# Attention weights on ScalarE: each half's logarithm followed at once by that half's two exponentials

## The chip, the cores and the metric

The kernel runs on one core of a Trainium2 chip. The metric is the device time of one execution in microseconds (us), given as the median of several runs of the same kernel. A profile of one execution stands beside it: the trace shows when each engine worked, what it worked on and what ended its waits.

## What is computed

The program takes x of 16 sequences, 256 tokens and 128 channels through four layers, each behind a layer norm and with a residual: a Mamba block, a mixture of experts, an attention, and the experts again. The change lies in the attention. It has 16 heads of 8 channels and weighs keys by inverse squared distance, not by a softmax:

```python
sq = q2 + jnp.swapaxes(k2, -1, -2) - 2.0 * jnp.einsum('bhqd,bhkd->bhqk', Q, K)
dist = jnp.sqrt(jnp.maximum(sq, 0.0))
W = (SHEP_EPS + dist) ** (-SHEP_P)          # SHEP_EPS = 1e-4, SHEP_P = 2
W = W / (SHEP_EPS + jnp.sum(W, axis=-1, keepdims=True))
return jnp.einsum('bhqk,bhkd->bhqd', W, V)
```

So for each of the 16 sequences there are 16 heads times 256 times 256 numbers to go through a square root and a power of -2. The kernel takes the power as exp(-2 ln(dist + eps)).

## The kernel before, in words

The layers run one after the other, with a barrier of all engines between them. Each engine has its own instruction list, written out by hand; what sets the order between engines are semaphores, and within an engine the order of the code.

The attention layer handles one sequence (a batch in the code) per turn, 16 turns, in a software pipeline. While turn b runs, TensorE (PE) computes the scores of the 16 heads of sequence b+1, one head at a time (`score`, L1295), into two PSUM buffers `s_ps`. VectorE (DVE) reads each into SBUF as a squared distance (`distance`, L1461), in the buffer `d`, which has two halves p and 1-p for alternate sequences. After heads 7, 11 and 15 DVE raises `d_ready`. ScalarE (ACT) meanwhile turns the distances of sequence b, which lie in the other half of `d`, into weights, in place. PE multiplies finished weights by the values (`weigh`, L1303), four heads at a time: the weighing of the first three groups stands in PE's list behind the scores of heads 13, 14 and 15, and that of the fourth behind head 1 of the next turn. Each waits for one more count of `w_done`, which ACT raises once per finished group. What follows (transposes L1312 and L1318, the division by the sum and the gate on DVE, the output projection L1324, the update of x at L1497) is spread over the heads of the next turn.

ACT's work of one turn is short: three square roots (heads 0 to 7, 8 to 11, 12 to 15; L1384), a load of the function table that holds both logarithm and exponential (L1385), two logarithms of 8 heads each (L1388), and four exponentials of 4 heads each (L1392), each of which raises `w_done`. The table of the square root is loaded again at the head of the next turn. ACT signals itself with `act_chain`: the three square roots raise it to 3, the two logarithms to 5, and an instruction that reads what an earlier one wrote waits for that count. On ACT no DMA is issued in this layer.

For the last sequence there are no further scores to compute: PE does the four groups, then two rounds of transposes and the projection, and the layer ends with DVE's update of x.

Another place that the prediction uses is the softplus of the Mamba layer (L486 to L488): three ACT instructions in a row, of which each reads what the one before it wrote and waits for its semaphore.

Of the kernel before, what the change touches and what calls it, by code (L numbers as in the profile page):

```python
# [23 lines left out]
ACT = mybir.ActivationFunctionType  # L24
# [14 lines left out]
HG = 4  # L39
# [24 lines left out]
def take(eng, sem, n=1):  # L64

    eng.wait_ge(sem, n)
    eng.sem_inc(sem, -n)  # L67
# [1034 lines left out]
def attention_layer(nc, sems, x_sb, aw, loaded, ident, ident16, half):  # L1102

    ctx = ExitStack()
    with ctx:
# [6 lines left out]
        def sem(name):  # L1112
            return sems.enter_context(nc.semaphore("a_" + name))
# [38 lines left out]
        pool_chain, dve_chain, act_chain, d_chain = sem("pool_chain"), sem("dve_chain"), sem("act_chain"), sem("d_chain")  # L1152
# [4 lines left out]
        s_ready, s_free, d_ready, w_done = sem("s_ready"), sem("s_free"), sem("d_ready"), sem("w_done")  # L1157
# [3 lines left out]
        def batches(eng, body, prologue, epilogue):  # L1161


            prologue()
            body(-1, 1, core=False, tail=False)
            body(0, 0, tail=False)
            with eng.Fori(0, NB // 2 - 2) as i:
                body(i * 2 + 1, 1)
                body(i * 2 + 2, 0)
            body(NB - 3, 1, further=False)  # L1170
            body(NB - 2, 0, further=False, ahead=False)
            body(NB - 1, 1, further=False, ahead=False, heads=False)
            epilogue()
# [10 lines left out]
        @block.sync  # L1184
        def _(sp):
            sp.wait_ge(loaded["attention"], 16 * len(aw.NAMES))
            for s in w_ready.values():
                sp.sem_inc(s, 1)
# [184 lines left out]
        @block.scalar  # L1373
        def _(act):
            def body(b, p, core=True, tail=True, heads=True, ahead=True, further=True):

                def heads_of(first, n):
                    return d[:, p, first:first + n].rearrange("p h k -> p (h k)")

                if not core:  # L1380
                    return
                for first, n in ((0, 8), (8, 4), (12, 4)):
                    take(act, d_ready)
                    nc.scalar.activation(heads_of(first, n), heads_of(first, n), ACT.Sqrt).then_inc(act_chain, 1)  # L1384
                nc.scalar.preload_act_table_set("natural_log_exp_and_others")  # L1385
                for half in range(2):
                    act.wait_ge(act_chain, 1 + 2 * half)
                    nc.scalar.activation(heads_of(8 * half, 8), heads_of(8 * half, 8), ACT.Ln, bias=near[:, 0:1]).then_inc(act_chain, 1)  # L1388
                for g in range(HG):
                    if g % 2 == 0:  # L1390
                        act.wait_ge(act_chain, g // 2 + 4)
                    nc.scalar.activation(heads_of(4 * g, 4), heads_of(4 * g, 4), ACT.Exp, scale=-2.0).then_inc(w_done, 1)  # L1392
                act.sem_inc(act_chain, -5)

            act.wait_ge(near_made, 1)
            batches(act, body, lambda: None, lambda: None)
# [262 lines left out]
```

## Time and profile before

| what | us |
|---|---|
| runs, median | 1593.68 |
| runs, all three | 1593.68, 1592.61, 1593.71 |
| the profiled execution, device time | 1592.62 |
| its span in the profile | 1590.9 |
| busy in that span: PE | 1308.6 |
| DVE | 1273.3 |
| ACT | 1097.2 |
| POOL (GpSimd) | 897.1 |

The span runs from the first instruction of the program to the last; 1.7 us of the device time lie around it. The shares of busy time are means over four layers that are limited by different things. The attention layer lies at about 850 to 1278 us of the span, between the two expert layers.

### The profile page before, as it was taken

Reading aid. Unit: us, or ns where it says so; the run is one execution under the profiler, and the core shown is the slowest. Engines: PE = TensorE matmul, PEld = TensorE weight load, DVE = VectorE, ACT = ScalarE, POOL = GpSimd, SP = SyncE. Lnnn points to the kernel's source line nnn. Section 1 sums busy time; section 2 is a strip of 40 time slices with the busy share of each in tenths; the row PEclk is TensorE's granted clock in tenths of the full one; section 3 lists DMA queues with packets and bytes.
Section 4 is the critical chain, followed back from the end, with each engine's and each line's share of the span. In section 5 each row is a group of like instructions: output and inputs, shape, how many; then the busy total and the mean of one; then the engine's idle time right before and its main releaser. Section 6 shows DMA issues by size and latency. Waiting matters only on the chain. (4 is left out here: it accounts for less than half of the span.)

```text
span 1590.9 us, 21353 instructions
## 1 busy us (share of the span) xinstructions
PE 1308.6 (82%) x6384; PEld 626.4 (39%) x6384; DVE 1273.3 (80%) x2163; ACT 1097.2 (69%) x1578; POOL 897.1 (56%) x1052
## 2 busy tenths in 40 slices
PE   4688888888886499999994777778878569999998
PEld 3344444444442244444441233333333224444443
DVE  2899999999999678878864788888887357877775
ACT  4667767867866255555550899999999935555554
POOL 5898888889877365555554322322321025555555
PEclk8899999999999799999996577867766569999999
DMA  7122122122110132222220000000000022223330
GB/s 239 54 80 81 53 71 88 53 69 91 53 70 37 77 137 108 107 106 106 106 107 0 1 1 0 0 0 0 0 0 1 1 107 114 114 113 126 149 149 35
DMA packets 27923, 111.54 MB, mean 70 GB/s; under 512 B 4049, under 2 KB 9570, under 8 KB 19426
## 3 DMA queue, kind: packets, MB, share of 16 engines
q1 hardware_dynamic: 27010, 110.21, 18.5%
q10 hardware_dynamic: 864, 0.74, 0.1%
q8 instruction: 22, 0.36, 0.1%
q14 instruction: 27, 0.22, 0.0%
HBM read 108.06 MB, written 2.88 MB: 70 GB/s over the span
## 5 line engine op out<-in xcount | busy, mean ns | idle before, releaser
L845 POOL TENSOR_TENSOR e_h_lo<-e_h,e_h_hi 128x512 f16<-128x512 f32 x272 | 314.7, 1157 | 273.3 <-ACT e_h_hi L961 262.2
L270 POOL TENSOR_TENSOR m_h<-m_b_sb,m_dx 128x512 f32<-128x512 f32 x256 | 345.0, 1374 | 49.1 <-POOLq L67 40.4
L498 ACT ACTIVATE m_decay<-m_delta,mw_a_log 128x255 f32<-128x255 f32 x448 | 185.3, 461 | 119.4 <-DVEq L648 119.2
L643 DVE TENSOR_TENSOR_SCAN m_h<-m_decay,m_h 128x1024 f32<-128x1024 f32 x112 | 255.8, 2284 | 13.2 <-DVEq L60 7.5
L1056 DVE TENSOR_TENSOR e_cu<-e_u,e_c_bc 128x512 f32<-128x512 f32 x256 | 175.9, 687 | 108.7 <-PE e_u L885 87.5
L956 ACT ACTIVATE e_g<-e_g 128x512 f32<-128x512 f32 x256 | 149.1, 582 | 162.8 <-PE e_g L885 162.8
L374 PE MATMUL m_y_ps<-m_hc,ident 128*128 128x512 f32 x512 | 250.4, 613 | 0.0
L885 PE MATMUL e_g<-e_x_hi,ew_gate_up 128*128 128x512 f16 x544 | 210.2, 386 | 9.4 <-ACTq L960 9.4
L1461 DVE TENSOR_SCALAR a_d<-a_s 128x512 f32<-128x512 f32 x256 | 170.3, 686 | 56.7 <-PE a_s L1295 36.8
L885 PE MATMUL e_u<-e_x_hi,ew_gate_up 128*128 128x512 f16 x544 | 209.2, 385 | 0.0
L892 PE MATMUL e_y<-e_h_hi,ew_down 128*128 128x512 f16 x544 | 206.9, 381 | 1.6 <-POOL e_h_lo L845 1.6
L961 ACT ACTIVATE e_h_hi<-e_h 128x512 f16<-128x512 f32 x272 | 169.5, 623 | 55.7 <-DVE e_h L1061 54.9
L1061 DVE TENSOR_TENSOR e_h<-e_g,e_cu 128x512 f32<-128x512 f32 x256 | 176.9, 691 | 15.9 <-DVE e_cu L1056 1.1
L598 DVE TENSOR_TENSOR m_hc<-m_h,m_c_ps 128x1024 f32<-128x1024 f32 x128 | 152.8, 1194 | 0.6 <-PE m_c_ps L369 0.6
L1295 PE MATMUL a_s<-a_qkT 32*128 32x256 f16 x512 | 105.6, 341 | 57.7 <-DVE a_d L1461 42.8
L374 PEld LDWEIGHTS m_y_ps<-m_hc,ident 128*128 128x128 f32 x512 | 92.8, 197 | 73.0 <-issue 70.4
L1384 ACT ACTIVATE a_d<-a_d 128x2048 f32<-128x2048 f32 (+1 forms) x48 | 115.7, 2469 | 5.7 <-ACTq L67 5.5
L369 PE MATMUL m_c_ps<-m_bc,m_pick 96*128 96x256 f16 x256 | 49.4, 274 | 83.0 <-DVE m_hc L598 72.4
L1388 ACT ACTIVATE a_d<-a_d,a_near 128x4096 f32<-128x4096 f32 x32 | 116.9, 3701 | 0.2
L1392 ACT ACTIVATE a_d<-a_d 128x2048 f32<-128x2048 f32 x64 | 116.7, 1894 | 0.0
L885 PE MATMUL e_g<-e_x_lo,ew_gate_up 128*128 128x512 f16 x272 | 105.1, 386 | 0.0
L885 PE MATMUL e_u<-e_x_lo,ew_gate_up 128*128 128x512 f16 x272 | 104.6, 385 | 0.0
(190 smaller groups left out, 1999.5 us busy)
## 6 DMA issues: line engine op xcount, KB each, us to landing
e_c_bc<-mix SPq DMA_DIRECT2D x64, 1024.0 KB, 6.8
m_b_sb<-b_rows SPq DMA_DIRECT2D x64, 512.0 KB, 5.4
ew_gate_up<-w_gate_up SPq DMA_DIRECT2D x1, 2176.0 KB, 13.5
out<-x_sb SPq DMA_DIRECT2D x8, 256.0 KB, 2.3
ew_down<-w_down SPq DMA_DIRECT2D x1, 1088.0 KB, 11.5
mw_conv_rows<-w_conv_rows ACTq DMA_DIRECT2D x1, 640.0 KB
mix<-e_cT SPq DMA_DIRECT2D x16, 32.0 KB, 1.6
x_sb<-x SPq DMA_DIRECT2D x1, 256.0 KB, 3.1
```

Of the source, the lines that this page charges most:

```text
L270: ins = nc.gpsimd.tensor_tensor(h[:, m % 4, :, c], b_sb[:, p, 2 * m:2 * m + 2], dx[:, p, c:c + 1].to_broadcast([P, 2, T]), ALU.mult)
L374: ins = nc.tensor.matmul(y_ps[:], ident[:], hc[:, m % 2, n].rearrange("p c t -> p (c t)"), start=(m == 0 and n == 0), stop=(m == PAIRS - 1 ...
L498: ins = nc.scalar.activation(decay_of(m, p)[:, at + 1:at + T], delta[:, p, c, 1:T], ACT.Exp, scale=neg_a[:, c, 2 * m + n:2 * m + n + 1])
L598: nc.vector.tensor_tensor(hc[:, m % 2], h[:, m % 4], c4, ALU.mult).then_inc(hc_ready, 1)
L643: nc.vector.tensor_tensor_scan(flat, decay_of(m, p)[:], flat, 0.0, ALU.mult, ALU.add).then_inc(scan_chain, 1)
L845: nc.gpsimd.tensor_tensor(h_lo[:, k], h[:, k], h_hi[:, k], ALU.subtract).then_inc(h_lo_ready, 1)
L885: ins = nc.tensor.matmul(ps[bank][:], ew.gate_up[r][:, e, side], a[:, p], start=(n == 0), stop=(n == 2))
L892: ins = nc.tensor.matmul(y_ps[:], ew.down[r][:, e], a[:, place(e)], start=(e == 0 and n == 0), stop=(e == NE and n == 2))
L961: nc.scalar.activation(h_hi[:, place(e)], h[:, place(e)], ACT.Copy).then_inc(h_hi_ready, 1)
L1056: nc.vector.tensor_tensor(cu[:, e % 2], u_ps[bank][:], c_bc[:, e], ALU.mult).then_inc(core_chain, 1)
L1061: nc.vector.tensor_tensor(h[:, place(e)], g_ps[bank][:], cu[:, e % 2], ALU.mult).then_inc(h_ready, 1)
L1461: ins = nc.vector.tensor_scalar(d[:, p, h], s_ps[h % 2][:], -2.0, 0.0, ALU.mult, ALU.max)
```

## The change

In each turn ACT issued logarithm 0, logarithm 1, exponentials 0, 1, 2, 3. Now it issues logarithm 0, exponentials 0 and 1, logarithm 1, exponentials 2 and 3. The instructions, their shapes, their number and the table loads are the same; only the place of the second logarithm among them is another. The counts of `act_chain` that are waited for stay: 4 (first logarithm done) ahead of exponential 0 and 5 (second logarithm done) ahead of exponential 2.

```diff
                 for half in range(2):
-                    act.wait_ge(act_chain, 1 + 2 * half)
+                    act.wait_ge(act_chain, (1, 3)[half])
                     nc.scalar.activation(heads_of(8 * half, 8), heads_of(8 * half, 8), ACT.Ln, bias=near[:, 0:1]).then_inc(act_chain, 1)
-                for g in range(HG):
-                    if g % 2 == 0:
-                        act.wait_ge(act_chain, g // 2 + 4)
-                    nc.scalar.activation(heads_of(4 * g, 4), heads_of(4 * g, 4), ACT.Exp, scale=-2.0).then_inc(w_done, 1)
+                    act.wait_ge(act_chain, 4 + half)
+                    for g in (2 * half, 2 * half + 1):
+                        nc.scalar.activation(heads_of(4 * g, 4), heads_of(4 * g, 4), ACT.Exp, scale=-2.0).then_inc(w_done, 1)
                 act.sem_inc(act_chain, -5)
```

ACT's list of one turn inside the loop, before; L1384 are the square roots, L1388 the logarithms, L1392 the exponentials, and `a_d` is the buffer `d`:

```order
L1384 ACT_TABLE_LOAD [waits a_d_ready]
L1384 ACTIVATE a_d<-a_d 128x4096
L1384 ACTIVATE a_d<-a_d 128x2048 [waits a_d_ready] x2
L1385 ACT_TABLE_LOAD
L1388 ACTIVATE a_d<-a_d,a_near 128x4096 [waits a_act_chain] x2
L1392 ACTIVATE a_d<-a_d 128x2048 [waits a_act_chain]
L1392 ACTIVATE a_d<-a_d 128x2048
```

The other two exponentials follow there in the same form. The same turn after the change, where the exponentials are line 1391:

```order
L1384 ACT_TABLE_LOAD [waits a_d_ready]
L1384 ACTIVATE a_d<-a_d 128x4096
L1384 ACTIVATE a_d<-a_d 128x2048 [waits a_d_ready] x2
L1385 ACT_TABLE_LOAD
L1388 ACTIVATE a_d<-a_d,a_near 128x4096 [waits a_act_chain]
L1391 ACTIVATE a_d<-a_d 128x2048 [waits a_act_chain]
L1391 ACTIVATE a_d<-a_d 128x2048
L1388 ACTIVATE a_d<-a_d,a_near 128x4096 [waits a_act_chain]
L1391 ACTIVATE a_d<-a_d 128x2048 [waits a_act_chain]
L1391 ACTIVATE a_d<-a_d 128x2048
```

The second logarithm has moved behind the first two exponentials, and each logarithm now stands directly ahead of an exponential that reads its result. No table load has come in.

PE's list at the end of the layer, for the last sequence, which the change leaves as it was:

```order
L1303 MATMUL a_av<-a_d,a_v 32x256 [waits a_v_ready,a_w_done]
L1303 MATMUL a_av<-a_d,a_v 32x256 x7
L1303 MATMUL a_av<-a_d,a_v 32x256 [waits a_w_done]
L1303 MATMUL a_av<-a_d,a_v 32x256 x7
L1303 MATMUL a_av<-a_d,a_v 32x256 [waits a_w_done]
L1303 MATMUL a_av<-a_d,a_v 32x256 x7
L1303 MATMUL a_av<-a_d,a_v 32x256 [waits a_w_done]
L1303 MATMUL a_av<-a_d,a_v 32x256 x7
L1312 MATMUL a_u<-ident,a_avT 128x128 [waits a_avT_ready]
```

The four groups wait for one count of `w_done` each, so the first two can now start when ACT has done half of the sequence, and the last two as before, behind the last two exponentials.

## Rows read from the trace of the kernel before

**Rows 1.** The page: span, and busy time with share and instructions of each engine.

```profile
span 1590.9 us, 21353 instructions
PE 1308.6 (82%) x6384; PEld 626.4 (39%) x6384; DVE 1273.3 (80%) x2163; ACT 1097.2 (69%) x1578; POOL 897.1 (56%) x1052
```

**Rows 2.** Busy time by stretch, the attention's steady part; columns in the first line.

```profile
core 0: us, PE busy (x) PEld busy (x) DVE busy (x) ACT busy (x) POOL busy (x), PEclk, DMA share, GB/s
890.00:1265.00 375.00, 287.32 (x1958) 123.27 (x1959) 293.83 (x649) 374.10 (x170) 97.93 (x219) 0.70 0.00 0
```

**Rows 3.** Timeline of ACT, one turn: start, duration, operation, count, idle before it.

```profile
930.69 7.22 ACT L1384 ACTIVATE a_d<-a_d 128x4096 f32<-128x4096 f32 x3
...
939.22 7.31 ACT L1388 ACTIVATE a_d<-a_d,a_near 128x4096 f32<-128x4096 f32 x2
946.43 7.29 ACT L1392 ACTIVATE a_d<-a_d 128x2048 f32<-128x2048 f32 x4
953.75 1.28 ACT L1384 ACT_TABLE_LOAD   x1
```

**Rows 4.** Groups by shape on ACT: count, busy us, mean ns of one, idle before.

```profile
L1388 ACT ACTIVATE a_d<-a_d,a_near 128x4096 f32<-128x4096 f32 x32 | 116.9, 3701 | 0.2
L1392 ACT ACTIVATE a_d<-a_d 128x2048 f32<-128x2048 f32 x64 | 116.7, 1894 | 0.0
...
L488 ACT ACTIVATE m_sp<-m_sp 128x512 f32<-128x512 f32 x16 | 10.1, 631 | 0.5
```

**Rows 5.** Timeline of ACT in the Mamba layer: one softplus, its two dependent instructions.

```profile
32.81 0.63 ACT L487 ACTIVATE m_sp<-m_sp 128x512 f32<-128x512 f32 x1
33.47 0.63 ACT L488 ACTIVATE m_sp<-m_sp 128x512 f32<-128x512 f32 x1
```

**Rows 6.** Waits, 900 to 1270 us: who for whom, us in total, times, longest.

```profile
PE a_av L1303 <- ACT a_d L1392: 14.1, 6, 9.4
```

**Rows 7.** Timelines of ACT and DVE, second turn: third square root and its input.

```profile
906.33 7.22 ACT L1384 ACTIVATE a_d<-a_d 128x4096 f32<-128x4096 f32 x3
...
908.27 0.69 DVE L1461 TENSOR_SCALAR a_d<-a_s 128x512 f32<-128x512 f32 x1 [0.23 <-PE a_s L1295]
```

**Rows 8.** Timeline, end of the attention layer: the last sequence on ACT, PE and DVE.

```profile
1255.81 7.31 ACT L1388 ACTIVATE a_d<-a_d,a_near 128x4096 f32<-128x4096 f32 x2
1263.03 7.29 ACT L1392 ACTIVATE a_d<-a_d 128x2048 f32<-128x2048 f32 x4
1264.97 5.11 PE L1303 MATMUL a_av<-a_d,a_v 128*32 128x256 f32 x48 [9.40 <-ACT a_d L1392]
...
1270.37 1.07 PE L1303 MATMUL a_av<-a_d,a_v 128*32 128x256 f32 x16 [0.29 <-ACT a_d L1392]
...
1272.46 1.06 PE L1312 MATMUL a_u<-ident,a_avT 128*128 128x128 f32 x8 [1.02 <-PEq L67]
...
1275.38 0.41 PE L1318 MATMUL a_u<-ident,a_o 128*128 128x128 f32 x2 [1.85 <-PEq L67]
...
1276.51 1.19 PE L1324 MATMUL a_u<-aw_attn_out_w,a_oT 128*128 128x128 f32 x4 [0.72 <-PEq L67]
```

**Rows 9.** Busy time by stretch at that end; granted TensorE clock stands behind POOL.

```profile
1268.00:1270.00 2.00, 2.00 (x24) 0.57 (x16) 0.69 (x1) 2.00 (x2) 0.00 (x0) 0.62 0.00 0
1270.00:1272.00 2.00, 1.15 (x20) 0.42 (x16) 0.38 (x1) 0.32 (x1) 0.00 (x0) 1.00 0.00 0
...
1276.00:1278.00 2.00, 1.19 (x4) 0.93 (x4) 0.40 (x2) 0.00 (x0) 0.00 (x0) 0.59 0.04 8
```

**Rows 10.** Timeline of PE: the same work at the other clock, in earlier turns.

```profile
915.40 1.94 PE L1312 MATMUL a_u<-ident,a_avT 128*128 128x128 f32 x8 [0.90 <-PEq L67]
...
974.06 0.68 PE L1324 MATMUL a_u<-aw_attn_out_w,a_oT 128*128 128x128 f32 x4
...
1143.21 1.93 PE L1303 MATMUL a_av<-a_d,a_v 128*32 128x256 f32 x16 [0.86 <-ACT a_d L1392]
...
1253.00 0.66 PE L1318 MATMUL a_u<-ident,a_o 128*128 128x128 f32 x2 [1.85 <-PEq L67]
```

## The prediction, made before the changed kernel was run

> **What bounds the kernel now.** The busy shares of the whole span come first, and they mislead: PE has 82%, DVE 80%, ACT 69% [rows 1]. The change touches one layer, so the second view is the busy time of that layer's steady stretch, 890 to 1265 us. There ACT works 374.10 of 375.00 us, DVE 293.83 and PE 287.32 [rows 2]: ACT bounds the attention, and its 0.9 us of idle time are small gaps around table loads. No DMA runs there (share 0.00). The third view is ACT's timeline over one turn [rows 3]: three square roots from 930.69, two logarithms from 939.22, four exponentials from 946.43, the next turn's table load right behind them at 953.75. The reader is to see that nothing between these rows is a wait for another engine; the turn of 24.35 us repeats to the end of the layer. The fourth view is who waits for ACT: PE waits at the weighing, 14.1 us in 6 waits, of which one of 9.4 is that of the last sequence [rows 6, 8]. So PE and DVE have time to spare in each turn and ACT has none. What the change does to ACT's own sequence is paid in full, and what it gives PE earlier is worth something only where PE makes ACT wait, or at the end of the layer.
>
> **The change part by part.** *What stays.* The 32 logarithms, 64 exponentials and 48 square roots, their shapes and the two table loads of a turn are the same, and the order of the changed program shows no load between a logarithm and an exponential. In the trace of before one load (L1385) already serves both [rows 3]. These edits cost nothing. The constant pair that replaces a formula gives the same counts.
>
> *What is added: two dependent starts in a turn.* Before, each logarithm was followed by an instruction that did not need it: logarithm 0 by logarithm 1, logarithm 1 by exponential 0, which reads what logarithm 0 wrote 3.6 us earlier. Now exponential 0 reads what the instruction directly ahead of it writes, and so does exponential 2. Behind these waiting instructions are queued on ACT the rest of the turn and all later turns.
>
> The price of an independent start: two logarithms take 7.31 us from the first start to the last end, and the exponential starts 946.43 - 939.22 = 7.21 us after the first start, so it starts 0.1 us ahead of the end of its predecessor [rows 3]. More sharply by sums: 32 logarithms of 3.701 us would fill 118.4 us, and they cover 116.9; 1.5 us over the 16 pairs is 0.096 us of overlap. The exponentials say the same: 64 times 1.894 is 121.2, they cover 116.7; 4.5 us over the 48 pairs is 0.094 [rows 4]. The price of a dependent start: in the softplus L488 reads what L487 wrote, and starts 33.47 - (32.81 + 0.63) = 0.03 us after its end [rows 5]; over 16 of them the idle time before L488 is 0.5 us, 0.031 each [rows 4]. That is the same engine, the same kind of instruction and the same way of waiting; only the size differs, 512 elements against 4096. So a dependent start costs 0.094 + 0.031 = 0.125 us more than an independent one. Two in each of 16 turns are 32, or **4.0 us on the path**. Bounds from the same rows: 32 x 0.094 = 3.0 if nothing but the overlap were lost, and 0 if a long instruction told its successor earlier than a short one does. I take 4.0, since both parts of it repeat through all their rows.
>
> *What is removed: PE's wait for the first weights.* Exponential 0 ends some 3.6 us earlier in the turn (a logarithm's 3.701 less an overlap), and with it the first two groups can be weighed earlier. On the path this is worth nothing as long as ACT is never short of distances. The tightest place is the second turn: DVE finishes head 15 at 908.27 + 0.69 = 908.96, and the third square root, which needs it, starts 7.22 - 1.89 = 5.33 us after 906.33, at 911.66 [rows 7, 4]. There are 2.7 us of slack, and the change can only widen them: PE reaches the scores of heads 14 and 15 behind weighings that now wait less. What is late next is the third group, whose exponential comes no earlier than before. PE's waits move to there: nothing gained, nothing lost.
>
> *The end of the layer.* Here the last sequence has a tail that nothing hides. The last exponential ends at 1263.03 + 7.29 = 1270.32 and PE begins the fourth group at 1270.37 [rows 8]: no backlog of the first three groups is left, so starting two of them earlier shortens nothing. But it moves PE's work, and PE's granted clock moves with it. Before, the three groups ran in one piece from 1264.97 (48 matmuls, 5.11 us); the clock was at 0.5 of full, 1.2 GHz, and rose within the slice 1268 to 1270, to 2.4 GHz from 1270 on; it fell within 1276 to 1278 [rows 8, 9]. So the fourth group (1.07 us), the transposes (1.06) and the two that follow (0.41) ran at the higher clock and the projection (1.19) at the lower. After the change the first two groups run about 3.6 us earlier, PE then rests until the third group is ready, and the rise may come later. If it comes too late for all three, they cost 1.93, 1.94 and 0.66 us [rows 10], that is 0.86 + 0.88 + 0.25 = 2.0 us more, and the fourth group starts 0.1 us later, since the slow third (1.93) outlasts the 1.8 us between two exponentials [rows 4]: +2.1. If the rise comes as before, 0. If a later rise also means a later fall, the projection takes 0.68 instead of 1.19 [rows 10]: -0.5. I take the middle case, in which the third and the fourth group run slowly (+1.0) and the later fall gives the projection back (-0.5): **+0.5 us**, with the ends -0.5 and +2.1.
>
> The sum against the profiled execution: 1592.62 + 4.0 + 0.5 = 1597.1 us. The runs of before lie at two levels, 1592.6 and 1593.7; the profiled execution is of the lower, the median 1593.68 of the upper, which gives 1598.2. I take the middle, **1597.7 us**, 4.5 us above the middle of the two levels.
>
> **The rivals.** *No cost for a dependent start* (not slower). If the overlap of a long logarithm does not depend on who reads it, or if ACT is told of the write before its end shows, the 4.0 us vanish and the time is 1592.6 to 1593.7, or up to 2.1 more with a slow tail. For it speaks only that no logarithm of 4096 elements is followed by its reader in the trace of before; against it the even 0.031 and 0.094 us [rows 4, 5]. It decides as soon as the cost of one start falls below 0.1 us: 32 of them are then within 3.2 us, which is 0.2% and about what a measurement of this kernel can tell from no change.
> The Trainium skill, in Advanced Engine Details and Errata under The Read-Write Bubble, says that on ScalarE the memory latency stands as a bubble between any two instructions, reader or not; by that rule the dependent start adds nothing, the sum is this rival's, and the trace disagrees, with 0.094 us of overlap in the one case and 0.031 of gap in the other.
>
> *PE sets the pace* (faster). If ACT's turns were in truth drawn along by PE's waits at the weighing, the waits other than the last sequence's, 14.1 - 9.4 = 4.7 us [rows 6], would go, and ACT's extra starts would lie in gaps: 1593.2 - 4.7 = 1588.5 us. It would need gaps on ACT ahead of its square roots. There are none in the steady stretch [rows 2, 3], so this has a small chance.
>
> *A cold tail* (slower still). The end of the layer runs wholly at the lower clock, +2.1 instead of +0.5: 1592.6 + 4.0 + 2.1 = 1598.7 to 1599.8. For it speaks that PE rests twice in the last sequence instead of once; against it that the third and fourth group, both slow, would follow each other without a pause, as the three groups did before the rise [rows 8, 9].
> The Trainium skill, in TensorE: Matmul & The Clock Gate under Part 1, says that the clock follows how busy the array has been of late; it speaks for this rival, and rows 9 agree in that the rise came in the midst of unbroken matmuls.
>
> *A reload of the table* at each change between logarithm and exponential can be left out: none stands in the new order.
>
> **How the numbers follow.** The forecast has 0.70, the cold tail 0.13, a start that costs nothing or too little 0.13, PE's pace 0.04. The first two are slower by over 0.2%: 0.83. The third is within 0.2%, 0.13, and the last faster, 0.04. The range goes from the lower level with the best tail and 0.3 us of scatter, 1592.6 + 4.0 - 0.5 - 0.3 = 1595.8, to the upper with the cold tail and 0.4 of scatter, 1593.7 + 4.0 + 2.1 + 0.4 = 1600.2, and leaves the last two cases out.
>
> **What would show it.** In the profile of after: ACT's turn is 24.60 us instead of 24.35; each logarithm is followed by idle time of 0.03 us, and the extent of two exponentials in a row stays 3.69; the steady stretch lasts 4 us longer with ACT still near 100% busy; PE's waits at the weighing stand before the third group and not the first. In the tail, the fourth group takes 1.07 or 1.93 us. The prediction is wrong if ACT's turn stays within 0.1 us of 24.35, if ACT shows waits ahead of its square roots, or if the expert layer behind it begins otherwise than shifted.

## The result and the profile after

The changed kernel takes 1598.36 us (median of 7 runs, 1597.46 to 1599.30), the kernel before 1592.95 us in the runs beside it (7 runs, 1592.61 to 1593.71). The ratio is 1.0033 with a 95% interval of 1.0021 to 1.0045: 5.4 us slower. The profiled execution took 1598.36 us with a span of 1596.6 us, 5.7 us more than before [rows 1].

The first view is ACT's timeline over the same turn as in rows 3: start, duration, operation, count. Line 1388 is the logarithm, 1391 now the exponential.

```profile
929.99 1.28 ACT L1384 ACT_TABLE_LOAD   x1
931.28 7.22 ACT L1384 ACTIVATE a_d<-a_d 128x4096 f32<-128x4096 f32 x3
938.52 1.28 ACT L1385 ACT_TABLE_LOAD   x1
939.81 3.71 ACT L1388 ACTIVATE a_d<-a_d,a_near 128x4096 f32<-128x4096 f32 x1
943.55 3.71 ACT L1391 ACTIVATE a_d<-a_d 128x2048 f32<-128x2048 f32 x2
947.17 3.70 ACT L1388 ACTIVATE a_d<-a_d,a_near 128x4096 f32<-128x4096 f32 x1
950.90 3.71 ACT L1391 ACTIVATE a_d<-a_d 128x2048 f32<-128x2048 f32 x2
954.63 1.28 ACT L1384 ACT_TABLE_LOAD   x1
```

From load to load the turn is 954.63 - 929.99 = 24.64 us, where it was 24.35 [rows 3]. The square roots and the loads are as long as before. The exponentials start 0.03 us after the end of their logarithm (939.81 + 3.71 = 943.52, then 943.55), and two exponentials in a row take 3.71 us instead of 3.69.

The second view is the groups by shape on ACT in the attention layer: count, busy us and mean ns of one, idle time before.

```profile
L1391 ACT ACTIVATE a_d<-a_d 128x2048 f32<-128x2048 f32 x64 | 118.7, 1902 | 1.0
L1388 ACT ACTIVATE a_d<-a_d,a_near 128x4096 f32<-128x4096 f32 x32 | 118.5, 3702 | 0.2
```

The 32 logarithms now cover 118.5 us, the sum of their single lengths, where they covered 116.9 [rows 4]. That alone does not show a lost overlap: the cover of a group counts only what its own members share, and the logarithms no longer stand side by side. (They cover 118.5 us as well in the experiment below that has this order without the waits.) What shows it are the starts: before, the first exponential started 0.1 us ahead of the end of the second logarithm [rows 3]; now each exponential behind a logarithm starts after its end. Before the 64 exponentials stands 1.0 us of idle time, 0.031 at each of the 32 that read their predecessor's result, and the mean of one has grown from 1894 to 1902 ns.

The third view is the busy time of the steady stretch, with the columns of rows 2, and PE's waits at the weighing over 900 to 1275 us.

```profile
890.00:1265.00 375.00, 285.88 (x1954) 122.94 (x1954) 293.43 (x650) 373.12 (x168) 97.93 (x219) 0.71 0.00 0
```

```profile
PE a_av L1303 <- ACT a_d L1391: 24.0, 17, 7.3
```

ACT is still busy for 373.12 of 375 us. PE's waits did not go away. There are more of them, 24.0 us in 17 waits, where there were 14.1 in 6 up to 1270 us [rows 6], and a look at one later turn shows where they now stand (timeline of PE, weighing alone):

```profile
1142.92 1.94 PE L1303 MATMUL a_av<-a_d,a_v 128*32 128x256 f32 x16
1145.32 1.51 PE L1303 MATMUL a_av<-a_d,a_v 128*32 128x256 f32 x16
1149.96 1.07 PE L1303 MATMUL a_av<-a_d,a_v 128*32 128x256 f32 x16 [1.82 <-ACT a_d L1391]
1151.76 1.07 PE L1303 MATMUL a_av<-a_d,a_v 128*32 128x256 f32 x16 [0.40 <-ACT a_d L1391]
```

The first two groups go through unheld, the third waits 1.82 us and the fourth 0.40. Before, the wait stood ahead of the first group [rows 10]. It does not leave that place everywhere: in five turns the first group waited before, and in two it still does, for 0.44 and 0.92 us.

The fourth view is the end of the layer, against rows 8 and 9: the last sequence on ACT, PE and DVE, and the granted clock by slices (it stands behind POOL's column). PEq and DVEq are the engines' own sequencers.

```profile
1271.17 3.71 ACT L1391 ACTIVATE a_d<-a_d 128x2048 f32<-128x2048 f32 x2
1273.13 3.35 PE L1303 MATMUL a_av<-a_d,a_v 128*32 128x256 f32 x32 [3.74 <-ACT a_d L1391]
...
1277.51 1.07 PE L1312 MATMUL a_u<-ident,a_avT 128*128 128x128 f32 x8 [1.03 <-PEq L67]
...
1280.43 0.66 PE L1318 MATMUL a_u<-ident,a_o 128*128 128x128 f32 x2 [1.85 <-PEq L67]
...
1281.81 1.19 PE L1324 MATMUL a_u<-aw_attn_out_w,a_oT 128*128 128x128 f32 x4 [0.72 <-PEq L67]
...
1283.26 0.42 DVE L1496 TENSOR_TENSOR x_sb<-a_u,x_sb 128x256 f32<-128x256 f32 x1 [1.60 <-DVEq L67]
```

```profile
1268.00:1270.00 2.00, 1.40 (x16) 0.39 (x8) 0.41 (x1) 2.00 (x1) 0.00 (x0) 0.72 0.00 0
1270.00:1272.00 2.00, 0.00 (x0) 0.00 (x0) 0.28 (x1) 1.97 (x2) 0.00 (x0) 1.00 0.00 0
1272.00:1274.00 2.00, 0.86 (x10) 0.41 (x14) 0.00 (x0) 2.00 (x2) 0.00 (x0) 0.64 0.00 0
1274.00:1276.00 2.00, 2.00 (x24) 0.78 (x20) 0.00 (x0) 0.88 (x1) 0.00 (x0) 0.51 0.00 0
1276.00:1278.00 2.00, 0.97 (x15) 0.52 (x6) 0.69 (x1) 0.00 (x0) 0.00 (x0) 1.00 0.00 0
1278.00:1280.00 2.00, 0.58 (x6) 0.34 (x4) 1.17 (x4) 0.00 (x0) 0.00 (x0) 0.84 0.00 0
```

The last exponential ends at 1271.17 + 3.71 = 1274.88 us instead of 1270.32 [rows 8]; the first logarithm of the layer started at 890.53 us and 890.51 before. So ACT's part of the layer is 4.54 us longer. From there the last update of x ends 1283.68 - 1274.88 = 8.80 us later; before it was 8.06. That makes 4.54 + 0.74 = 5.3 us. The other 0.4 us of the span's 5.7 lies in the last expert layer, which has nothing changed: from the last update of x to the end of the span there were 312.5 us before, 312.9 after, and between 312.8 and 313.3 in the traces of the experiments.

### The profile page after: what moved, and what is told of

The parts are those of the page before. It is cut to its first block and busy times, and to the rows that moved or that the text cites. A ratio compares the mean times of both kernels' runs of the same rounds, so it can differ in the third digit from the quotient of the medians.

```text
span 1596.6 us, 21353 instructions
## 1 busy us (share of the span) xinstructions
PE 1306.3 (82%) x6384; PEld 624.4 (39%) x6384; DVE 1273.1 (80%) x2163; ACT 1100.6 (69%) x1578; POOL 897.0 (56%) x1052
## 5 line engine op out<-in xcount | busy, mean ns | idle before, releaser
L1384 ACT ACTIVATE a_d<-a_d 128x2048 f32<-128x2048 f32 (+1 forms) x48 | 115.7, 2469 | 5.7 <-ACTq L67 5.5
L1391 ACT ACTIVATE a_d<-a_d 128x2048 f32<-128x2048 f32 x64 | 118.7, 1902 | 1.0
L1388 ACT ACTIVATE a_d<-a_d,a_near 128x4096 f32<-128x4096 f32 x32 | 118.5, 3702 | 0.2
L1303 PE MATMUL a_av<-a_d,a_v 128*32 128x256 f32 x1024 | 87.7, 474 | 24.0 <-ACT a_d L1391 24.0
```

## The experiments

The theory after this reading: the loss is the **dependent start**, an ACT instruction that waits for the one directly ahead of it. Two in a turn cost 0.284 us, 16 turns 4.54 us. The rival: it is the **new order**, through the moment at which PE gets weights, its clock, or anything else that moves with it. A third term is the end of the layer. The kernel before was run on the same chips beside each set: 1593.23 us (26 runs) for the first four experiments, 1592.27 us (21 runs) for the last two.

### The waits without the order

```diff
                 for half in range(2):
-                    act.wait_ge(act_chain, 1 + 2 * half)
+                    act.wait_ge(act_chain, 1 + 3 * half)
                     ...
                 for g in range(HG):
                     if g % 2 == 0:
-                        act.wait_ge(act_chain, g // 2 + 4)
+                        act.wait_ge(act_chain, 5)
```

> The order of before (both logarithms, then four exponentials), but logarithm 1 waits for logarithm 0 and exponential 0 waits for logarithm 1: two starts per turn that wait for their direct predecessor, with PE's work in the order and at the places of before. Theory 1 (the loss is the dependent start, 0.143 us each as the changed kernel's turn of 24.64 us against 24.35 shows): ACT's turn becomes 24.64 us, the layer 16 x 0.29 = 4.6 us longer, the end of the layer (last exponential to the last update of x) stays at 8.1 us as before; 1592.9 + 4.6 = 1597.5 us. Theory 2 (the loss comes from the new order: weights that are ready earlier move PE's work and its clock, and ACT's waits cost nothing): the turn stays at 24.35 us and the time at 1592.9.

Measured: 1597.40 us, ratio 1.0029 (1.0017 to 1.0040), 4.2 us over before. The timeline of ACT, one turn:

```profile
929.72 1.28 ACT L1384 ACT_TABLE_LOAD   x1
...
939.54 7.45 ACT L1388 ACTIVATE a_d<-a_d,a_near 128x4096 f32<-128x4096 f32 x2
947.03 7.31 ACT L1392 ACTIVATE a_d<-a_d 128x2048 f32<-128x2048 f32 x4
954.36 1.28 ACT L1384 ACT_TABLE_LOAD   x1
```

The turn is 24.64 us, as in the changed kernel, with PE's work where it was before. Two logarithms take 7.45 us instead of 7.31 [rows 3], and the first exponential starts after the end of the second and not ahead of it. The order is not needed for the loss; the waits alone make it. Nor is the reading needed: logarithm 1 works on other heads than logarithm 0, exponential 0 reads what logarithm 0 wrote, and neither touches what its direct predecessor writes. The cost comes with the wait for the direct predecessor.

### One dependent start instead of two

```diff
...
+                log(0)
+                act.wait_ge(act_chain, 4)
+                power(0)
+                log(1)
+                power(1)
+                act.wait_ge(act_chain, 5)
+                power(2)
+                power(3)
```

`log(half)` is one logarithm with its wait for the square roots, `power(g)` one exponential; these lines stand in the place of both loops, which are left out here.

> Order logarithm 0, exponential 0, logarithm 1, exponentials 1, 2, 3: exponential 0 still reads its direct predecessor, exponential 2 no longer does (exponential 1 stands between). One dependent start per turn instead of two. Theory 1: turn 24.35 + 0.143 = 24.50 us, 16 x 0.143 = 2.3 us over before, plus 0 to 0.8 at the end of the layer: 1595.2 to 1596.0 us. Theory 2 (order): the first weights come as early as in the changed kernel, the second 1.8 us later than before less one logarithm; the loss would stay near that of the changed kernel, 1597 to 1598.5.

Measured: 1595.85 us, ratio 1.0016 (1.0007 to 1.0025), 2.6 us over before. ACT's timeline:

```profile
929.86 1.28 ACT L1384 ACT_TABLE_LOAD   x1
...
939.68 3.71 ACT L1388 ACTIVATE a_d<-a_d,a_near 128x4096 f32<-128x4096 f32 x1
943.43 1.91 ACT L1391 ACTIVATE a_d<-a_d 128x2048 f32<-128x2048 f32 x1
945.24 3.69 ACT L1388 ACTIVATE a_d<-a_d,a_near 128x4096 f32<-128x4096 f32 x1
948.84 5.50 ACT L1391 ACTIVATE a_d<-a_d 128x2048 f32<-128x2048 f32 x3
954.36 1.28 ACT L1384 ACT_TABLE_LOAD   x1
```

The turn is 24.50 us. Exponential 0 starts 0.04 us after its logarithm's end and takes 1.91 us; behind the second logarithm the next one starts ahead of the end, at 948.84 against 945.24 + 3.69 = 948.93. Half the dependent starts, half the growth of the turn.

### The order without the waits

```diff
-                    act.wait_ge(act_chain, (1, 3)[half])
-                    nc.scalar.activation(heads_of(8 * half, 8), heads_of(8 * half, 8), ACT.Ln, bias=near[:, 0:1]).then_inc(act_chain, 1)
+                    act.wait_ge(act_chain, 3 + half)
+                    nc.scalar.activation(aside[:], aside[:], ACT.Ln, bias=near[:, 0:1], scale=0.0).then_inc(act_chain, 1)
-                    act.wait_ge(act_chain, 4 + half)
                     for g in (2 * half, 2 * half + 1):
+                        if g == 3:
+                            act.wait_ge(act_chain, 5)
...
```

`aside` is a buffer of the logarithm's shape, which POOL fills once with ones (lines not shown). The kernel leaves out the power of -2: its logarithms work on `aside`, and its exponentials read the square roots.

> The order of the changed kernel (logarithm, two exponentials, logarithm, two exponentials), but the logarithms work on a buffer of their own of the same shape and the exponentials directly on the distances' roots, so that no instruction reads what its direct predecessor wrote; the power of -2 is left out (the weights are exp(-2 dist)). Same instructions and shapes, same moment of the first weights. Theory 1: ACT's turn is back at 24.35 us and the time at 1592.9 plus 0 to 0.8 for the end of the layer, 1592.9 to 1593.7 us. Theory 2 (order): turn and time stay as in the changed kernel, 1597.5 to 1598.4 us.

Measured: 1594.31 us, ratio 1.0008 (0.9999 to 1.0017), 1.1 us over before, and the interval does not exclude that there is no change. It is 0.6 above the upper end that was expected; that end was counted from 1592.9, and from the 1593.23 of the runs beside it 0.3 remain. ACT's timeline and the end of the layer on PE:

```profile
928.79 1.28 ACT L1386 ACT_TABLE_LOAD   x1
...
938.61 3.71 ACT L1390 ACTIVATE a_aside<-a_aside,a_near 128x4096 f32<-128x4096 f32 x1
942.23 3.69 ACT L1394 ACTIVATE a_d<-a_d 128x2048 f32<-128x2048 f32 x2
945.83 3.69 ACT L1390 ACTIVATE a_aside<-a_aside,a_near 128x4096 f32<-128x4096 f32 x1
949.43 3.70 ACT L1394 ACTIVATE a_d<-a_d 128x2048 f32<-128x2048 f32 x2
953.14 1.28 ACT L1386 ACT_TABLE_LOAD   x1
```

```profile
1268.00 3.73 PE L1305 MATMUL a_av<-a_d,a_v 128*32 128x256 f32 x32 [3.83 <-ACT a_d L1394]
1272.75 1.94 PE L1314 MATMUL a_u<-ident,a_avT 128*128 128x128 f32 x8 [1.02 <-PEq L67]
1276.55 0.66 PE L1320 MATMUL a_u<-ident,a_o 128*128 128x128 f32 x2 [1.85 <-PEq L67]
1277.92 1.19 PE L1326 MATMUL a_u<-aw_attn_out_w,a_oT 128*128 128x128 f32 x4 [0.72 <-PEq L67]
```

The turn is back at 24.35 us in the order of the changed kernel: the order costs ACT nothing. What is left in the trace is the end of the layer. It is 10.1 us long here (last exponential's end to the last update of x), because third and fourth group, transposes and projection all ran at the lower clock (0.50 in every slice of 2 us from 1268 on): 3.73 us for the two groups, 1.94 for the transposes that took 1.06 before [rows 8]. That is the cold tail of the prediction's rivals, 2.0 us in this one execution. The 0.8 us that I had put as the most for this term was too little.

### The end of the layer by itself

The last sequence is a turn of its own in the code, so it can have the one order and all others the other. First the changed kernel with the old order in the last turn:

```diff
+                if heads:
+                    for half in range(2):
                     ...
+                else:
+                    for half in range(2):
                     ...
+                    for g in range(HG):
```

Under `if heads` stands the changed code, for all turns but the last, and under `else` the code of before.

> The changed kernel, but the last sequence alone in the order of before. Theory 1 with the end of the layer as a term of its own: the tail from the last exponential's end to the last update of x goes from 8.80 back to about 8.06 us, and two dependent starts (0.29 us) go as well: 1598.4 - 0.74 - 0.29 = 1597.4 us. If the end of the layer has no part in the loss, only the 0.29 goes: 1598.1 us. PE's weighing of the last sequence then stands in one piece again, with the rise of the clock inside it.

Measured: 1597.19 us, ratio 1.0027 (1.0017 to 1.0038), 4.0 us over before, where the changed kernel is 5.4 over it. PE at the end of the layer:

```profile
1270.00 6.47 PE L1303 MATMUL a_av<-a_d,a_v 128*32 128x256 f32 x64 [9.73 <-ACT a_d L1400]
```

All four groups stand in one piece again (x64), and the tail from the last exponential (1268.05 + 7.29 = 1275.34) to the last update of x (1282.53 + 0.42 = 1282.95) is 7.6 us. Then the reverse, the kernel before with the new order in the last turn only:

> The kernel before, with the last sequence alone in the order of the changed kernel. Two dependent starts (0.29 us) in the last turn, and the tail from the last exponential's end to the last update of x should be that of the kernels whose last sequence has the new order (8.8, 8.9 and 10.1 us in the three traces so far) and not that of the old order (8.1, 7.6, 7.6): 1593.2 + 0.3 + 0.7 to 2.4 = 1594.2 to 1595.9 us. If the tail's length is chance and not the order's, it is 7.6 to 8.1 here and the time within 0.5 us of before. ACT's turn stays at 24.35 us for all but the last.

Measured: 1594.22 us, ratio 1.0012 (1.0003 to 1.0021), 1.95 us over before. In the trace:

```profile
1267.13 3.71 ACT L1400 ACTIVATE a_d<-a_d 128x2048 f32<-128x2048 f32 x2
1269.09 3.42 PE L1303 MATMUL a_av<-a_d,a_v 128*32 128x256 f32 x32 [3.66 <-ACT a_d L1400]
...
1279.29 0.42 DVE L1505 TENSOR_TENSOR x_sb<-a_u,x_sb 128x256 f32<-128x256 f32 x1 [1.60 <-DVEq L67]
```

The tail is 8.9 us (1267.13 + 3.71 = 1270.84 to 1279.29 + 0.42 = 1279.71). Over all traces: with the old order in the last turn 8.1 (before), 7.6, 7.6 and 7.7 us; with an order that lets the first group go ahead 8.8 (after), 8.9, 8.9 and 10.1 us. The two sets do not overlap, which speaks for the order and against chance: 0.7 to 2.5 us. The runs agree in direction, 1.4 us less and 1.95 us more, with 0.3 us of each being the two dependent starts of that turn. Only the second is clear of no change; the intervals of the first and of the changed kernel overlap. The intervals are as wide as the term, and its size is known from eight single traces only.

### Fewer starts

If ACT alone sets the turn, starts should be worth something in the other direction too. This kernel keeps the order of before, with two square roots of 8 heads in all turns but the first and two exponentials of 8 heads in all turns but the last:

```diff
+                roots = ((0, 8), (8, 8)) if tail else ((0, 8), (8, 4), (12, 4))
                 ...
+                n = 8 if heads else 4
+                for first in range(0, NH, n):
                     ...
+                    nc.scalar.activation(heads_of(first, n), heads_of(first, n), ACT.Exp, scale=-2.0).then_inc(w_done, n // 4)
```

> The order of before with fewer and wider instructions on ACT: two exponentials of 8 heads instead of four of 4 in all turns but the last, and two square roots of 8 heads instead of three in all but the first. If ACT alone sets the turn, each start that goes gives back what the rows price it at: two exponentials of 2048 start 1.800 us apart, a square root of 4096 holds ACT 3.524 us until the next start, so 0.076 us each; three starts less are 0.228 us per turn, 24.35 becomes 24.125, and 15 times 0.152 plus 15 times 0.076 is 3.4 us: 1593.2 - 3.4 = 1589.8 us. If the later first weights (the first two groups come together, 1.8 us later for the first) hold PE up until ACT lacks distances, the turn stays above 24.2 and ACT shows idle time ahead of its second square root.

Measured: 1588.26 us against 1592.27, ratio 0.9976 (0.9967 to 0.9985), 4.0 us faster than before, where 3.4 was expected: the fastest kernel of this study. ACT's timeline:

```profile
904.35 1.28 ACT L1385 ACT_TABLE_LOAD   x1
905.64 7.12 ACT L1385 ACTIVATE a_d<-a_d 128x4096 f32<-128x4096 f32 x2
...
921.30 7.11 ACT L1395 ACTIVATE a_d<-a_d 128x4096 f32<-128x4096 f32 x2
928.42 1.28 ACT L1385 ACT_TABLE_LOAD   x1
929.72 3.62 ACT L1385 ACTIVATE a_d<-a_d 128x4096 f32<-128x4096 f32 x1
933.51 3.62 ACT L1385 ACTIVATE a_d<-a_d 128x4096 f32<-128x4096 f32 x1 [0.17 <-ACTq L67]
```

The turn is 928.42 - 904.35 = 24.07 us, 0.28 less than before, where 0.23 was expected. From the first logarithm to the end of the last exponential ACT takes 375.9 us (890.01 to 1265.89), 3.9 less than the 379.8 before (890.51 to 1270.32). The expectation took its wide instruction, 3.524 us until the next start, from square roots behind a table load, which last 3.618. The wide exponentials, behind a running predecessor, last 3.601 on the mean:

```profile
L1395 ACT ACTIVATE a_d<-a_d 128x4096 f32<-128x4096 f32 x30 | 106.6, 3601 | 0.0
```

With the overlap of 0.094 that is 0.093 us for each start that goes, and 0.28 for three. The second square root had to wait for distances once, 0.17 us in the third turn, and in no other: that is how close ACT now runs behind DVE at the start of the layer.

## Why the prediction was right

**What bounds the layer.** Right. ACT is busy through the steady stretch in both traces, and a change of 0.28 us in its turn came out 16 times at the end of the layer (4.54 us). The wider instructions show the same with the other sign.

**The dependent start.** Right in kind, half a microsecond too small in size: 4.0 us predicted, 4.54 measured in the trace. The two parts that were priced came as priced: the overlap of 0.094 us goes, and a gap of 0.031 us comes [rows 4, 5]. What the step left out is that an instruction which starts without overlap is itself longer: 1.91 us instead of 1.89 for an exponential, which the group's mean shows too, 1902 against 1894 ns where half of them are concerned. So a dependent start costs 0.094 + 0.031 + 0.016 = 0.141 us, and 32 make 4.5. I could have read it before the run: square roots that followed idle time in the first turn took 1.91 us as well. One of them, in the trace of before:

```profile
881.59 1.91 ACT L1384 ACTIVATE a_d<-a_d 128x2048 f32<-128x2048 f32 x1 [1.74 <-ACTq L67]
```

That the price does not depend on the width was a guess from 512 elements, and it held for an exponential of 2048 and a logarithm of 4096 behind a logarithm of 4096.

**What PE gets earlier.** Right: worth nothing within the turns, as the turn of 24.35 us in the new order without the waits shows. The wait moved from the first group to the third in most turns that have one, as said, and also to the fourth, which was not said: a third group that is held until its exponential is done leaves 0.4 us to the next one.

**The end of the layer.** Right in sign, +0.5 predicted and +0.74 in the trace of after, but the nearness of the two is partly luck. Of the middle case one half came: third and fourth group ran mostly at the lower clock (0.51 in 1274 to 1276), and the fourth ended 1.60 us after the last exponential instead of 1.12. The other half did not: the clock fell again within 1278 to 1280, ahead of the two transposes of L1318, which took 0.66 instead of 0.41 us, and the projection stayed at 1.19. So the terms are +0.48 for the groups where +1.0 was put, +0.25 for the transposes where nothing was put, and 0 for the projection where -0.5 was put: errors that nearly cancel. The rise did not come once and later, as assumed, but twice: within 1268 to 1270, when the first two groups were nearly through, to be lost again in PE's rest by the slice 1272 to 1274, and a second time about the end of the fourth group (0.51 in 1274 to 1276, 1.00 in 1276 to 1278).

**The rivals.** A dependent start that costs nothing is excluded by the waits in the old order (24.64 us) and the new order without them (24.35 us). PE as the pace is excluded by the same pair, since PE's work had the old places in the one and the new in the other. The cold tail did not come in the profiled run of after, but did in that of the order without the waits, so its place in the range was deserved.

**The sum.** 1597.7 us predicted, 1598.36 measured; 4.5 us over the two levels' middle predicted, 5.4 us over the runs beside it measured. The missing 0.9 is the 0.54 of the dependent starts, 0.24 of the tail, and a remainder of 0.1 that no run tells from scatter. The two levels on which the middle was taken were three runs' chance: the 26 runs of before beside the experiments fill the space between, 1592.06 to 1594.22.

## What to carry to other kernels

On an engine that is never idle, the order of its own instructions has a price: put an independent instruction between one that is waited for and the one that waits, even where both orders have the same work, and do not let an instruction wait for its direct predecessor where it need not. Handing results over sooner pays only if someone who waits for them is on the path; here the one who waited was PE, which had 4.7 us of waits to lose and none that anyone waited for. Where such an engine bounds a stage, fewer and wider instructions can be a gain: here three starts less per turn gave 4.0 us.

## What the hardware showed that I had not expected

An ACT instruction's own duration depends on how it starts: 1.89 us behind a running predecessor, 1.91 us behind an idle moment, for the same 128x2048 exponential or square root. The logarithm of 128x4096 lasts 3.69 us behind a running exponential and 3.71 behind a table load. And PE's higher clock can be spent on nothing: in the trace of after it was granted when the first two groups of the last sequence, 3.6 us at the lower clock, were nearly through, stood at 1.00 in 1270 to 1272 us, a slice without a single matmul, and was down again while the third and fourth group ran.
